# Mamba halves as a three-item pipeline, and PSUM split into 4 + 3 + 1 banks, in a one-core decoder layer

## What is computed

```python
out1 = mamba(rmsnorm(x, w1));  x1 = x + out1
out2 = mamba(rmsnorm(x1, w2)); out2 = memory_attend(out2)
x = layernorm(x + x1 + out2)
x = layernorm(x + cross_attention(x, context))      # 16 heads, 64 context rows
x = layernorm(x + layernorm(x + moe(x)))            # 8 experts, top 2
```

```python
xm, res = split(x @ in_w.T + in_b)
xm = silu(conv4(xm) + conv_b)
delta = softplus((xm @ xp_w.T)[:, :64] @ dt_w.T + dt_b)
h = h * exp(delta * A) + (delta * xm) * B_t         # a state of 512 x 16, token by token
y = sum_n(h * C_t) + xm * D;  y = y * silu(res);  return y @ out_w.T + out_b
```

## Time and profile before

| what | value |
|---|---|
| time, median of 3 runs | 3658.72 us (3632.02 to 3663.42) |
| the profiled execution: its time | 3660.78 us |
| the profiled execution: its span | 3659.0 us |
| busy | PE 75%, PEld 56%, DVE 61%, ACT 52%, POOL 46% |
| mean granted clock of TensorE | 0.90 of full speed |

### The profile page before, as it was taken

How to read it: one execution, slowest core, us unless ns; L and a number is a source line. 1 busy time by engine, 2 the same in 40 slices (tenths; PEclk the granted TensorE clock), 3 DMA queues, 4 the chain that set the end, 5 groups by cost and what they waited for, 6 DMA issues and landing times.

```text
span 3659.0 us, 44328 instructions
## 1 busy us (share of the span) xinstructions
PE 2742.5 (75%) x15274; PEld 2050.4 (56%) x15275; DVE 2217.9 (61%) x2787; ACT 1904.8 (52%) x3028; POOL 1665.2 (46%) x1723
## 2 busy tenths in 40 slices
PE   5787688877777896687688867777895299999910
PEld 2674576547647754674676547647754166666600
DVE  4894893468668645894893468678643033333347
ACT  5785781378678525785781378678531011111100
POOL 2792791039639602792791039639602501000060
PEclk9898899889989998898899889989996599999955
DMA  5110120001001100110110001001102212111031
GB/s 197 43 51 1 41 64 1 12 18 52 25 18 50 38 1 13 44 50 1 44 61 1 12 18 53 24 18 53 35 1 102 81 62 90 62 63 62 33 93 47
DMA packets 91235, 158.84 MB, mean 43 GB/s; under 512 B 14130, under 2 KB 39986, under 8 KB 91058
## 3 DMA queue, kind: packets, MB, share of 16 engines
q1 hardware_dynamic: 72338, 106.80, 9.4%
q0 software_dynamic: 15392, 47.99, 3.6%
q10 hardware_dynamic: 3328, 1.76, 0.2%
HBM read 118.36 MB, written 38.14 MB: 43 GB/s over the span
## 4 chain that ended last, share of the span: by engine, by line
PE 41%; POOL 30%; DVE 11%; issue 8%; ACT 7%; DMA 2%; another core or an unknown queue 1%; DVEq 0%; POOLq 0%; SPq 0%; ACTq 0%
POOL arena L597 25%; PE psD L926 13%; PE psD L1237 7%; PE psA L926 6%; POOL arena L582 4%; PE psD L1114 2%; PE psA L1089 2%; PE psD L1135 2%; DVE arena L1351 2%; PE psA L973 2%; PE psA L1228 1%; DVE arena L1349 1%; PE psA L920 1%; ACT arena L779 1%; DVE arena L1338 1%
## 5 line engine op out<-in xcount | busy, mean ns | idle before, releaser
L597 POOL TENSOR_TENSOR arena<-arena 128x512 f32<-128x512 f32 x1024 | 1091.2, 1092 | 10.7 <-POOL carry L593 0.5
L1012 PE MATMUL psD<-ident,arena 128*128 128x128 f32 x4096 | 651.6, 286 | 274.6 <-ACT arena L779 209.9
L1012 PEld LDWEIGHTS psD<-ident,arena 128*128 128x128 f32 x4096 | 479.1, 146 | 374.0 <-ACT arena L779 273.5
L786 ACT ACTIVATE arena<-arena,negA 128x512 f32<-128x512 f32 x1024 | 662.1, 712 | 12.2 <-DVE arena L1363 11.4
L1363 DVE TENSOR_TENSOR_SCAN arena<-arena,psD 128x512 f32<-128x512 f32 x512 | 581.7, 1200 | 137.8 <-PE psA L1032 81.4
L1032 PE MATMUL psA<-ident,arena 128*128 128x128 f32 x4096 | 617.7, 274 | 19.0 <-POOL arena L597 18.7
L1363 DVE TENSOR_TENSOR_SCAN arena<-arena,carry,psD 128x512 f32<-128x512 f32 x512 | 602.4, 1255 | 37.0 <-PE psA L1032 37.0
L779 ACT ACTIVATE arena<-arena,bc 128x512 f32<-128x512 f32 x768 | 498.0, 712 | 87.4 <-PE psD L1012 86.3
L1032 PEld LDWEIGHTS psA<-ident,arena 128*128 128x128 f32 x4096 | 479.1, 142 | 32.3 <-POOL arena L597 32.3
L926 PE MATMUL psD<-arena 128*128 128x512 f32 (+4 forms) x776 | 336.9, 569 | 43.5 <-POOL strip L545 28.7
L883 ACT ACTIVATE in_w_sb<-in_w_sb 128x512 f32<-128x512 f32 x140 | 88.1, 630 | 457.6 <-DVE in_w_sb L1559 457.6
(11 more groups left out here) (202 smaller groups left out, 3527.6 us busy)
## 6 DMA issues: line engine op xcount, KB each, us to landing
arena<-c_dram SPq DMA_DIRECT2D x256, 256.0 KB, 3.2
arena<-in_W POOLq DMA_DIRECT2D x16, 1024.0 KB, 7.5
xs_dram<-zeros SPq DMA_DIRECT2D x40, 256.0 KB, 6.5
arena<-xs_dram SPq DMA_DIRECT2D x71, 128.0 KB
ys_dram<-arena POOLq DMA_DIRECT2D x70, 128.0 KB, 2.0
arena<-in_x SPq DMA_DIRECT2D x4, 1024.0 KB, 7.0
arena<-in_b POOLq DMA_DIRECT2D x8, 512.0 KB, 7.9
out<-arena SPq DMA_DIRECT2D x4, 1024.0 KB
```

Source lines behind the costliest of these rows:

```text
L597: pool.tensor_tensor(h_ring[:, r % H_SLOTS, :], h_ring[:, r % H_SLOTS, :], c_rows[:, (half * NS + n) % C_SLOTS, :], ALU.mult).then_inc(c_w ...
L786: act.activation(da_ring[:, r % DA_SLOTS, :], dt[:, f, half * HALF:(half + 1) * HALF], ACT.Exp, scale=negA[:, f, n:n + 1]).then_inc(da_rea ...
L1012: mm = pe.transpose(psD[:, r % RING, j * P:(j + 1) * P], g[:, (r // KI) % 2, j, f * P:(f + 1) * P], ident[:, :])
```

## The change

The block of 1024 tokens is cut into items: a batch has 4 (block 0 half 0, block 0 half 1, block 1 half 0, block 1 half 1), each with 64 chunks. One loop over steps c, from -64 to 256 + 20, is written on every engine. At step c = 64 s + r the engine works on chunk r of item s, and also, at fixed values of r, on a piece of the end of item s - 1 and a piece of the preparation of item s + 1. In steps -64 to -1 there is only the preparation of item 0, in the last 64 chunks no preparation, in the last 20 steps only the end of item 3. The second block's item needs only the same half of the first block, which ended a slot earlier.

- PSUM: psA keeps 4 banks for y. psD gives 3 banks to the scan's input and one bank (`bg_bank`) to all the other work of the pipeline: every job claims it after the previous job was drained, be it by ACT or DVE.
- Rings: 6 slots of decays (8 before), 8 of h. The distances (2, 6, 4, 4) stay.
- Preparation and end are done per half: every operation is 512 columns wide, and there are twice as many.
- Softplus: per channel tile, in successive steps, |z| and exp, and a step later the slope and the logarithm. `soft_ln`, `series` and `is_small` have 2 slots, so slope and logarithm wait for `replaced` and `dt_ready` of two tiles earlier. POOL now does the comparison of all tiles (DVE did two of four).
- The reciprocal root of the mean square is Ln and Exp (-0.5) on ACT instead of Sqrt on ACT and a reciprocal on DVE. The normalisation moves to POOL.
- `spread_b` on ACT: the three tiles stand in three successive steps, not together.
- x1 is made in place in xin, and x is loaded again into `base` after the blocks; POOL has one more addition of 2048 columns there. At the end of the program the load of the first batch's x2 waits for the last norm.

The core of the diff. The loop over c stands four times, once per engine; below are its start and ACT's pieces, then those of PE, then those of DVE:

```diff
-        RUN = 2 * CHUNKS
-        DA_SLOTS = H_SLOTS = 8
-        C_SLOTS = 4
+        ITEMS = 4
+        RUN = ITEMS * CHUNKS
+        TAIL = 20
+        DA_SLOTS, H_SLOTS, C_SLOTS = 6, 8, 4
+        FILL_BANKS = 3
+        TURN = [8, 10, 12, 14]
+        MO = [10, 12, 14, 16]
+        XNT = [22, 23]
+        IN = [25, 27, 29, 31]
+        GATE = [26, 28, 30, 32]
+        XD = [38]
+        BCT = [40]
+        Z = [41, 42, 43, 44]
+        UT = [50, 51, 52, 53]
+        KEEP_Y = 6
+        PADS, XB = 2, 1
+        SQUARE = [MO[j] + 2 for j in range(JT)]
+        RMS, NORM = 19, 20
+        SILU = 36
+        SOFT = [z + 2 for z in Z]
...
+        def when(c):
+            s, r = divmod(c, CHUNKS)
+            items = [q if 0 <= q < ITEMS else None for q in (s - 1, s, s + 1)]
+            return (r, *items)
...
+                def claim_bg(name, i, j):
+                    q = bg_at[name, i, j][0]
+                    if q >= 1:
+                        by, count = bg_jobs[q - 1]
+                        pe.wait_ge(bg_by_act if by == "act" else bg_by_dve, count)
...
+                def fill(c):
...
+                    if c >= FILL_BANKS:
+                        pe.wait_ge(scanned, b * RUN + c - FILL_BANKS + 1)
...
+                def find_rms(i):
+                    act.wait_ge(squares, JT * (i + 1))
+                    act.activation(inv_rms[:, 0, :], mean_sq[:, :], ACT.Ln, scale=1.0 / D, bias=eps_sb[:, 0:1]).then_inc(inverse, 1)
...
+                    act.activation(inv_rms[:, 1, :], inv_rms[:, 0, :], ACT.Exp, scale=-0.5).then_inc(inverse, 1)
...
+                def decline(i, f):
...
+                    act.activation(soft_e[:, f, :], dt[:, i % 2, f, :], ACT.Abs).then_inc(soft_abs, 1)
...
+                    act.activation(soft_e[:, f, :], soft_e[:, f, :], ACT.Exp, scale=-1.0).then_inc(soft_exp, 1)
...
+                def slope(i, f):
...
+                        act.wait_ge(replaced, n - 1)
+                    act.activation(series[:, f % 2, :], soft_e[:, f, :], ACT.Copy, scale=1.0 / 3.0, bias=-0.5)\
...
+                        act.wait_ge(dt_ready, n - 1)
+                    act.activation(soft_ln[:, f % 2, :], soft_e[:, f, :], ACT.Ln, bias=1.0).then_inc(soft_log, 1)
...
+                def soften(i, f):
...
+                    pool.tensor_scalar(is_small[:, f % 2, :], soft_e[:, f, :], SMALL_E, None, ALU.is_lt)\
...
+                    pool.tensor_tensor(series[:, f % 2, :], series[:, f % 2, :], soft_e[:, f, :], ALU.mult)\
...
+                for c in range(-CHUNKS, RUN + TAIL):
+                    r, k, s, p = when(c)
+                    if 0 <= c + DECAY_AHEAD < RUN:
+                        decay(c + DECAY_AHEAD)
...
+                    if p is not None and r == SILU:
+                        silu_conv(i0 + p)
+                    if s is not None and r == SILU:
+                        silu_gate(i0 + s)
...
+                    if p is not None and r in SOFT:
+                        decline(i0 + p, SOFT.index(r))
+                    if p is not None and r - 1 in SOFT:
+                        slope(i0 + p, SOFT.index(r - 1))
...
+                    if 0 <= c + FILL_AHEAD < RUN:
+                        fill(c + FILL_AHEAD)
+                    if 0 <= c - SUM_AFTER < RUN:
+                        add_y(c - SUM_AFTER)
+                    if k is not None and r in MO:
+                        leave(i0 + k, MO.index(r))
+                    if k is not None and r in TURN:
+                        turn_y(i0 + k, TURN.index(r))
...
+                    if 0 <= c < RUN:
+                        scan(c)
...
+                            for tap in range(1, TAPS):
+                                if r == IN[f] + 1 + tap:
+                                    convolve(i0 + p, f, tap)
...
+                            if r == SOFT[f] + 2:
+                                expand(i0 + p, f)
+                            if r == SOFT[f] + 3:
+                                replace(i0 + p, f)
+                            if r == SOFT[f] + 4:
+                                finish_dt(i0 + p, f)
+                            if r == SOFT[f] + 5:
+                                times_u(i0 + p, f)
```

More of the change, by code:

```diff
@@ new lines, in decoder_layer @@
+        bg_at, drains = {}, {"act": [], "dve": []}
+        bg_jobs = []
+        for b in range(B):
+            for slot_at in range(-1, ITEMS + 1):
+                for r in range(CHUNKS):
+                    for name, times, shift, by in STAGES:
+                        if r in times and 0 <= slot_at + shift < ITEMS:
+                            drains[by].append(len(bg_jobs))
+                            bg_at[name, b * ITEMS + slot_at + shift, times.index(r)] = (len(bg_jobs), len(drains[by]))
+                            bg_jobs.append((by, len(drains[by])))
@@ L612, in _ @@
+                pool.wait_ge(x_again, b * 16 + 16)
+                pool.wait_ge(bg_by_dve, taken("mo", i0 + ITEMS - 1, JT - 1))
+                pool.tensor_tensor(base[:, :, :], base[:, :, :], xin[:, :, :], ALU.add).then_inc(sum01, 1)
                 pool.wait_ge(sum01, b + 1)
@@ L1413, in _, with bg_wait, gate_y @@
             for b in range(B):
-                for m in range(2):
-                    mamba(b, m)
+                i0 = b * ITEMS
+                def bg_wait(name, i, j):
+                    dve.wait_ge(bg_full, filled(name, i, j))
+                    return psD[:, bg_bank(name, i, j), :]
+                def gate_y(i, j):
+                    if j == 0:
+                        dve.wait_ge(gate_ready, KI * (i + 1))
+                    bank = bg_wait("turn", i, j)
+                    dve.tensor_tensor(y[:, j % 2, :, :], bank.rearrange("p (k t) -> p k t", k=KI),
+                                      gate[:, :, j * P:(j + 1) * P], ALU.mult).then_inc(bg_by_dve, 1)
```

849 lines of the change are left out of this document (413 added, 436 removed).

## The result

| | before | after |
|---|---|---|
| median | 3654.35 us (5 runs, 3632.02 to 3663.42) | 3848.1 us (5 runs, 3844.61 to 3874.26) |
| profiled execution, span | 3659.0 us | 3872.8 us |
| mean granted clock | 0.90 | 0.865 |

The ratio is 1.0547 (95% interval 1.0497 to 1.0597): 194 us slower by the medians, where 89 were forecast. The two profiled executions lie 214 us apart; each was slower than its median, the one of the kernel after by 26 us. The sign was right, the size was not.

The account below looks back on a forecast made before the run. Scans were POOL's (154.3 of 164.3 us busy), the rest chains of engines taking turns. Per batch 327.9 + 56 + 25 + 165 = 573.9 against 552.8 us; four batches +84, x2 +5: 3750 profiled, 3748 median; range 3560 to 3880.

Parts of the forecast that it names:

- first preparation: Preparation of a batch's first half item, before any scan: 52.4 us, 56 with hand-offs; 43 low end, 65 high.
- x2's wait: First x2 load now starts with the other, whose wait was 16.75 us for twice the bytes: +5 of 0 to 8.
- The step that failed: POOL's cost per chunk in the scans: 1.07 us for the product with C, 0.17 for scaling by B, together 1.24.
- Steps 8 to 17 and 25 to 35: Item's end through one bank, +9 us (5 to 14); projections on PE with DVE's taps, +14 us (10 to 20).
- Steps 36 to 42: Silu of 8 tiles with two table loads, 6.8 us on ACT, then x_dbl on PE: +5 us (2 to 8).
- Steps 43 to 54, softplus: Largest term: ACT's 36.2 us against 15.4, with 8 table loads of 10.3 us per item: +23 us (18 to 30).
- Steps 0 to 7: Start of a slot: POOL's bias addition, +1 us in two slots.
- Costed at nothing: Three scan-input banks, six decay slots, ACT's separate scalings, reload of x with POOL's extra sum, SP's stores of C: no cost.
- the slot without a preparation: Last slot of a batch: end 9, gate projections 6 and Silu of the gate 1, 16 us added; some 98 us.
- Rival A: Logarithm's table serves the exponential in the new order: 29 to 32 us less per batch, 3630 us; chance 0.18.
- Rival B: DVE-POOL turns and one-bank waits feed on each other; 512-wide DVE operations over 1.3 us mean; 3870 us; chance 0.14.
- Rival C: Bursts overlap, slots cost ACT's busy 117 us, not 135; 3475 us in full, 3567 at two thirds; chance 0.26.

Follow-up runs that it names:

- two_bg: Kernel after with PSUM as 4 banks for y, 2 for scan input and 2 for background jobs, used in turn; ratio 1.0699 to the kernel before.
- gate_early: phase_table with B/C turning, dt projections and u transposes later or spread, and gate projections at steps 19, 20, 21, 24 instead of 26, 28, 30, 32; ratio 1.0200.
- late_best: phase_table with later places for turning B and C (42), dt projections (44, 45, 47, 48) and transposes of u (52, 53, 55, 56); ratio 1.0118.
- one_table: Kernel after with ACT naming a table set that serves Exp and Ln, at batch start and behind Silu; ratio 1.0496 to the kernel before.
- phase8: Kernel after with its C rows 8 bytes further on, so the product's operands differ by 8 modulo 16; ratio 1.0466 to the kernel before.
- late_after: Kernel after with later places for turning B and C, dt projections and transposes of u, as in late_best; ratio 1.0455 to the kernel before.
- phase_table: Kernel after with C rows and softplus series 8 bytes further on, and the table set serving Exp and Ln named; ratio 1.0227 to the kernel before.
- spread_soft: phase_table with softplus's channel tiles two steps apart (43, 45, 47, 49) and their products' transposes at 50, 52, 54, 56; ratio 1.0064.
- spread_cmp: spread_soft with softplus's comparison on DVE instead of POOL; ratio 1.0112 to the kernel before.
- micro: Separate kernel computing nothing of the layer, timing single operations on 128x512 SBUF tiles by operand offset, alone and beside other engines; POOL's product 1.26 or 1.09 us.
- before_series: Kernel before with softplus's exponentials 8 bytes further on, so the series' product's operands differ by 8 modulo 16; ratio 0.9994.

## Why the prediction was wrong

It forecast slower, for the reason that the added work doesn't fit beside the scans. That much held. Per batch it had 56 for the first preparation, 493 for the four slots, 25 for the end and 131 for attention, 705 us; measured were 65.0, 508.6, 27.9 and 133.1, 734 us. With x2's wait (26.7 us against 16.75, +10 where I took 5) that makes some 121 us over four batches, and the profiled execution is 124 us above the 3750 that were forecast for it. In the medians 100 of them show, since the profiled execution was the slowest of five. Its last stretch of 165.7 us, which took 134 in other profiles, may be the reason; the four other executions have no trace.

- *The step that failed* stands first in the working: "POOL: 1091.2 / 1024 = 1.07 us for the product with C", used for the kernel after as well, although every buffer was laid out anew. The new layout was costed at nothing, without being named. The runs showed 1.26 us for the new placement, and taking it away gives 15 us a batch by itself, of the 29 that the forecast lacks. Once the table sets are out of the way it gives 22 (721.5 to 699.8), the series' product included. It is the term that the sum lacks, and the largest.
- *First preparation*: 65 us against 56, my high end. This is the second largest. The working adds 3.6 us for hand-offs (52.4 to 56) to a chain whose jobs all go through one bank. With two background banks (two_bg) the same chain takes 57 us, so the single bank costs 8. PE's clock is low in both, 0.61 and 0.65, where it was 0.78 to 0.80; what the clock adds was not tested by itself.
- *Steps 8 to 17 and 25 to 35*, forecast at 21.8 and 28.1 us: 20.1, and 28.2 to 31.6. The sizes were about right, and in the projections so was the engine. But gate_early shows that a second limit stood right under the first. (PE's slack was read too high: 0.88 of 1.28 us leaves 30%, but its row in the scan stage has 131 of 164 us busy, which leaves 20%.)
- *Steps 36 to 42*: forecast 14, measured 16.6, 13.8 and 16.5. I had the Silu burst, but not that the fixed order puts four steps of other engines right behind it, nor the clock at 0.50 that follows; late_best takes 5.3 us off slot 0.
- *Steps 43 to 54, softplus*: forecast 38.4, measured 38.8, 37.3 and 38.8. The number was right by luck, its reason was not. I had ACT's loads as the limit with POOL and DVE under it. With the loads gone the stretch still takes 37.8: what else is in it, most likely DVE and POOL in turns and the waits of tiles that follow too closely, is as long.
- *Steps 0 to 7*: forecast 11.2, measured 14.1, 18.5 and 13.8. In slot 0 it is PE's clock: 13.04 of 14.11 us busy at 0.59, with POOL busy for 9.1 only. In one_table, phase8 and late_after two batches each have a clock of 0.69 to 0.94 there and take 12.1 us, with ACT busy throughout, and the other two 13.7 to 14.1 at 0.59 or 0.60. In slots 1 and 2 it is POOL, busy for 18.4 and 13.7 us; slot 1 has a bias addition of 2.37 us, where I had put 1, and slot 2 has none. In phase8 slot 1 falls to 15.3 in two batches and 17.5 in the other two, at a clock of 0.80; slot 2 doesn't fall.
- *Costed at nothing*: the slot without a preparation took 98.3 us, as forecast, but with POOL's longer product in it (95.7 in phase_table), so its other terms were some 3 us too high. two_bg shows what the third fill bank hides: with two, and two background banks, a slot loses 2 to 9 us.

Rival A's premise can be built (the trace has the loads gone) but not its price: 29 to 32 us a batch expected, 12 measured, 19 with the phase right (the series' product included). Rival B's turns are real, and its criterion was not met: the 28 operations have 1.01 us in the mean (taps 0.957), 0.36 of it waiting, as I had put. Its total of 3870 us came nearest, for another reason. Rival C, overlapping bursts, is refuted by the slots.

No variant that computes the whole layer beats the kernel before. The nearest by ratio is spread_soft (+0.6%) and not late_best (+1.2%), but on different chips: without the last stretch, from the first gather on, their profiles are 3527 and 3528 us long and that of the kernel before 3493, 1% for both. The nearest by batch period is spread_cmp, which draws level (685.1); its profile is 29 us longer than the one before for what lies outside the period, x2's wait (10 us) among it. Left open: what a second background bank is worth without giving up a fill bank, what a freer order of the pieces could still give, and what makes the clock fall after some gaps of PE and not after others.

## What to carry to other kernels

When buffers are laid out anew, compare the durations of the instructions that were not edited before reading anything else; here eight bytes cost the old kernel about as much as the whole change did. Where several engines are within a few per cent of each other in a stretch, a sum by the busiest may give the right number and the wrong cause: taking the supposed cost away shows it (here 1 us of 38.8), and costs are best taken away together as well as one by one. Before ranking variants measured on different chips, compare a stretch that no edit touches. A pipeline in program order should leave a few steps behind each burst before another engine needs its result.

## What the runs showed of the hardware

- POOL's tensor_tensor on 128x512 float32 takes 1.26 us when the addresses of its two SBUF inputs are equal modulo 16 and 1.09 when they differ by 8 (micro); for 128x1024, in softplus, 2757 against 2349 ns (before, before_series).
- A DVE tensor_scalar from SBUF to SBUF runs nearly in turns with POOL's product (0.48 us alone, 1.48 beside it), a scan with one input in PSUM does not (1.19 both ways).
- PE's granted clock fell to 0.50 (the lower of its two levels) after a gap of 2.88 us and stayed there for some 19 us of nearly full work; in late_best, after a gap of 3.34 us at the same place, it stayed at 1.00, and fell later in the softplus stretch (stages of late_best):

```profile
850.00:854.00 4.00, 0.66 (x7) 0.42 (x5) 3.32 (x3) 4.00 (x8) 3.26 (x5) 1.00 0.00 2
854.00:858.00 4.00, 4.00 (x30) 3.21 (x30) 2.44 (x2) 4.00 (x8) 1.86 (x2) 1.00 0.24 78
...
870.00:880.00 10.00, 4.79 (x20) 3.99 (x20) 10.00 (x9) 6.25 (x12) 10.00 (x8) 0.50 0.07 26
```
